# Moving borders between six mixers: an earlier first rounding of the second mixture call, a one-hot add at the end of the expert-choice mixer, and a new spread of jobs in a quaternion attention loop

## The reference

```python
x = x + 0.5 * _L0_ffn_ref(_layernorm(x), ...)    # top-2 of 7 experts, and a shared one
x = x + _L0_attn_ref(_layernorm(x), ...)         # 16 heads, 64 landmarks, 6 steps of an iterative inverse
x = x + 0.5 * _L0_ffn_ref(_layernorm(x), ...)
x = x + 0.5 * _L1_ffn_ref(_layernorm(x), ...)    # 16 experts choose their tokens, after 6 Sinkhorn steps
x = x + _L1_attn_ref(_layernorm(x), ...)         # quaternion projections, softmax attention
x = x + 0.5 * _L1_ffn_ref(_layernorm(x), ...)
```

```python
out = out.at[jnp.arange(b)[:, None, None], idx].add(gates[..., None] * expert_out)
```

## Time and profile before

| | us |
|---|---|
| median of 3 runs (lowest, highest) | 2918.04 (2917.66, 2918.88) |
| the profiled execution | 2915.34 |
| its span in the trace | 2913.6 |
| PE, DVE, ACT, POOL busy | 2781.3, 1843.2, 1635.9, 543.7 |

### The profile page before, as it was taken

How to read it: one execution, slowest core, us unless ns; L and a number is a source line. 1 busy time by engine, 2 the same in 40 slices (tenths; PEclk the granted TensorE clock), 3 DMA queues, 4 the chain that set the end, 5 groups by cost and what they waited for, 6 DMA issues and landing times.

```text
span 2913.6 us, 55420 instructions
## 1 busy us (share of the span) xinstructions
PE 2781.3 (95%) x22813; PEld 2168.1 (74%) x22813; DVE 1843.2 (63%) x3741; ACT 1635.9 (56%) x2473; POOL 543.7 (19%) x478
## 2 busy tenths in 40 slices
PE   9999999997999999999999978998999999998998
PEld 7889999996767778889999956995333434333998
DVE  7775555548887687755545477785635463436776
ACT  4534555543443355344545434775798878892776
POOL 0002224121000000022232254553000000001343
PEclk9999999998999999999999989999999999998999
DMA  4213333232000022233333354774442252513675
GB/s 157 71 66 124 83 87 98 70 86 73 2 2 24 3 69 80 66 113 92 85 84 87 79 155 128 206 201 104 98 131 54 71 112 64 124 38 119 190 205 139
DMA packets 237853, 279.72 MB, mean 96 GB/s; under 512 B 23811, under 2 KB 219040, under 8 KB 237600
## 3 DMA queue, kind: packets, MB, share of 16 engines
q1 hardware_dynamic: 205296, 228.75, 26.8%
q0 software_dynamic: 30720, 45.85, 8.1%
q10 hardware_dynamic: 1584, 1.57, 0.2%
HBM read 204.58 MB, written 72.88 MB: 95 GB/s over the span
## 4 chain that ended last, share of the span: by engine, by line
PE 74%; DVE 15%; ACT 5%; issue 4%; DMA 2%; POOL 1%; DVEq 0%; POOLq 0%; ACTq 0%
PE PS L162 17%; PE PS L163 16%; PE PS L164 16%; PE PS L2960 13%; PE PS L1043 6%; PE PS L170 2%; DVE SM L194 1%; ACT FW L556 1%; ACT Z L600 1%; DVE SM L1418 1%; PE PS L502 1%; DVE PROD L628 1%; DVE FW L640 1%; PE PS L3053 1%; PE PS L178 1%
## 5 line engine op out<-in xcount | busy, mean ns | idle before, releaser
L3110 ACT ACTIVATE P<-PS 128x1024 f32<-128x1024 f32 x512 | 484.9, 1046 | 94.8 <-PE PS L2960 93.1
L162 PE MATMUL PS<-FH,FW 128*128 128x366 f32 (+1 forms) x1408 | 506.5, 360 | 5.6 <-ACT SIL L542 4.3
L163 PE MATMUL PS<-FH,FW 128*128 128x366 f32 (+1 forms) x1408 | 497.5, 353 | 0.0
L164 PE MATMUL PS<-FH,FW 128*128 128x366 f32 (+1 forms) x1408 | 495.3, 352 | 0.0
L550 ACT ACTIVATE FHH<-PROD 128x366 fp32r<-128x366 f32 (+1 forms) x352 | 194.4, 552 | 424.1 <-DVE PROD L628 423.8
L162 PE MATMUL PS<-FW,FHH 128*122 128x256 f32 (+1 forms) x1184 | 337.8, 285 | 1.5 <-DVE FHH L635 1.5
L163 PE MATMUL PS<-FW,FHH 128*122 128x256 f32 (+1 forms) x1184 | 333.9, 282 | 0.0
L164 PE MATMUL PS<-FW,FHH 128*122 128x256 f32 (+1 forms) x1184 | 332.8, 281 | 0.0
L628 DVE TENSOR_TENSOR PROD<-SIL,PS 128x366 f32<-128x366 f32 (+1 forms) x352 | 206.9, 588 | 165.6 <-PE PS L164 155.8
L635 DVE TENSOR_TENSOR FHH<-PROD,FHH 128x366 fp32r<-128x366 f32 (+1 forms) x352 | 208.9, 594 | 147.4 <-ACT FHH L550 147.2
L162 PEld LDWEIGHTS PS<-FH,FW 128*128 128x128 f32 x1408 | 264.7, 188 | 30.5 <-ACT SIL L542 8.1
(11 more groups left out here) (468 smaller groups left out, 5562.4 us busy)
## 6 DMA issues: line engine op xcount, KB each, us to landing
WS<-L_ffn_w_dram SPq DMA_DIRECT2D x256, 256.0 KB, 3.7
WST<-L_ffn_W_dram SPq DMA_DIRECT2D x168, 256.0 KB, 3.4
S<-parts_scratch SPq DMA_DIRECT2D x60, 384.0 KB, 8.1
parts_scratch<-PT SPq DMA_DIRECT2D x28, 512.0 KB, 4.5
WST<-L_ffn_W1s_dram SPq DMA_DIRECT2D x40, 256.0 KB, 2.8
WST<-L_ffn_W3s_dram SPq DMA_DIRECT2D x40, 256.0 KB, 3.4
WST<-L_ffn_W2s_dram SPq DMA_DIRECT2D x40, 256.0 KB, 4.0
xa_scratch<-X SPq DMA_DIRECT2D x17, 512.0 KB, 5.1
```

The costliest lines, as they stand in the source:

```text
L162: e.matmul(o, lh, rh, start=start, stop=False, skip_group_check=True)
L163: e.matmul(o, ll, rh, start=False, stop=False, skip_group_check=True)
L164: return e.matmul(o, lh, rl, start=False, stop=stop, skip_group_check=True)
L3110: e.activation(self.PR[K % 3][:, 2 * jj:2 * jj + 2, :].rearrange("p a b -> p (a b)"), c.pair(2 * ((2 * K + jj) % 3)), ACT.Exp, scale=0.25) ...
```

## The change

**Opening.** X's first row group and the first weight piece are issued first, row groups 0, 2, 3 and 4 to 7 all on SP; g, b and the router's weights `WRF` move to ACT's queue. The 13 products of ones, 8 before the transposes and 5 behind, become 11 and 2.

**Second Ffn0 call.** `FW` gets a fixed place at the top of memory (the halves swap roles: `fw(q)` is half (q+1)%2), so it doesn't lie under tiles that Attn0 still uses; Attn0's `WP` moves. Seven pieces, no longer two, run ahead in Attn0's tail: loads and half of the statistics, the other half, root's first step, its other steps, the norm of rows 0 to 3, of rows 4 to 7, and the first weight rounding `wt 0` (between the last two and the last `le` items). The 2 products of ones before the second call's transposes go. `Z` and `FW` wait for batch 3's last use of what lay there (`rows_free`). g and b are not loaded a second time.

```diff
@@ Ffn0.order
-        self.ahead = [[("ld", n, 0), ("ld", n, 1), ("stats", n, 0, 4)], [("stats", n, 4, 8)]]
-        seq = [("consts", n), *self.ahead[0], *self.ahead[1], ("root", n, 0, 8)]
-        seq += [("norm", n, i, i + 4) for i in (0, 4)] + [("wt", n, 0), ("fill", n, 8 if self.first else 2)]
-        seq += [("tp", n, h, c) for h in range(2) for c in range(2)] + [("fill", n, 5 if self.first else 3), ("lg", n, 0)]
+        self.ahead = [[("ld", n, 0), ("ld", n, 1), ("stats", n, 0, 4)], [("stats", n, 4, 8)], [("root", n, 0, 8, 0)],
+                      [("root", n, 0, 8, 1)], [("norm", n, 0, 4)], [("norm", n, 4, 8)], [("wt", n, 0)]]
+        seq = [("consts", n)] + [it for piece in self.ahead for it in piece]
+        seq += [("fill", n, 11)] * self.first
+        seq += [("tp", n, h, c) for h in range(2) for c in range(2)] + [("fill", n, 2 if self.first else 3), ("lg", n, 0)]
@@ Attn0.__init__
-        self.rooms = ("lc", call, 3, 0, 0), ("le", call, 3, 3)
+        self.rooms = (("ib", call, 2, 0, 4), ("nd", call, 3, 1), ("ld", call, 2, 0, 0), ("iw", call, 3, 1), ("ld", call, 2, 1, 1),
+                      ("le", call, 2, 2), ("le", call, 3, 3))
+        c.rows_free = last(*values, *[("qk", call, 3, *x) for x in ALL4])
@@ macaron_kernel
-        parts.append((opens, begin[:5]))
+        parts.append((opens, begin[:3]))
-                own[:1] = [(ph, head[:3]), (opens, begin[5:]), (ph, head[3:])]
+                own[:1] = [(ph, head[:2]), (opens, begin[3:5]), (ph, head[2:3]), (opens, begin[5:]), (ph, head[3:])]
```

```diff
+            if not self.final and k == 59:
+                seq.append(("oh", n))
+            if not self.final and k == 61:
+                seq.append(("xget", n, 0))
...
-        return seq + [("end", n) if self.final else ("xget", n, 0)]
+        return seq + ([("end", n)] if self.final else [("hot", n, y) for y in range(4)])
@@ pe
+        elif k == "hot":
+            w.wait_ge(*p.at("oh", ("oh", n)))
+            w.wait_ge(*p.at("yev", ("ye", n, 15), 1))
+            for t in range(2):
+                o_ = 128 * (2 * it[2] + t)
+                ins = e.matmul(self.pb(it)[:, 256 * t:256 * t + 256], self.OH[0:64, o_:o_ + 128], self.YE[1][0:64, 0, :],
+                               start=True, stop=True, skip_group_check=True)
@@ dve
+        elif k == "hot":
+            w.wait_ge(*p.at("xl4" if y >= 2 else "xl0", ("xget", n, 0)))
+            w.wait_ge(*p.at("hp", it))
+            e.tensor_tensor(rows, rows, self.pb(it).rearrange("p (i d) -> p i d", i=2), ALU.add).then_inc(*p.one("hv"))
@@ sp, xget
-            w.wait_ge(*p.at(f"sc{b // 2}", ("sc", n, 15)))
+            w.wait_ge(*p.at(f"sc{b // 2}", ("sc", n, 15 if b else 14)))
```

```diff
@@ prep
+        to_rows, to_second, each_turned, each_query = {1: (8, 1, (2, 2, 2, 2), 2), 2: (4, 2, (1, 1, 1, 1), 1),
+                                                          3: (5, 1, (2, 1, 1, 1), 1)}[b]
-        q.add(5, ("zz", n, b, 0))
-        q.add(1, ("zz", n, b, 1), ("xb", n, b))
+        q.add(to_rows, ("zz", n, b, 0))
+        q.add(to_second, ("zz", n, b, 1), ("xb", n, b))
@@ sink_stats
-            q.add(1, *[("stats", self.call, b, b, i + x) for x in range(2)])
+            q.add(5 if b == 1 and not i else 1, *[("stats", self.call, b, b, i + x) for x in range(2)])
```

More of the change, by code:

```diff
@@ L198, in stats, with root @@
         ins.then_inc(*p.one("dv"))
-    def root(self, e, w, gs, done, by=1.0, more=EPS):
+    def root(self, e, w, gs, done, by=1.0, more=EPS, steps=(0, 1, 2)):
         p = self.p
@@ L205, in root @@
         w.wait_ge(*p.mine())
-        e.tensor_scalar(s1, self.MV[:, gs, 1], by, more, ALU.mult, ALU.add).then_inc(*p.one("dv"))
-        w.wait_ge(*p.mine())
-        e.tensor_scalar(s2, s1.bitcast(U32), -0.5, 1597463007.0, ALU.mult, ALU.add).then_inc(*p.one("dv"))
-        w.wait_ge(*p.mine())
-        e.tensor_copy(o.bitcast(U32), s2).then_inc(*p.one("dv"))
-        w.wait_ge(*p.mine())
-        for n in range(3):
+        if 0 in steps:
+            e.tensor_scalar(s1, self.MV[:, gs, 1], by, more, ALU.mult, ALU.add).then_inc(*p.one("dv"))
+            w.wait_ge(*p.mine())
+            e.tensor_scalar(s2, s1.bitcast(U32), -0.5, 1597463007.0, ALU.mult, ALU.add).then_inc(*p.one("dv"))
+            w.wait_ge(*p.mine())
+            e.tensor_copy(o.bitcast(U32), s2).then_inc(*p.one("dv"))
+            w.wait_ge(*p.mine())
+        for n in steps:
             e.scalar_tensor_tensor(s3, o, -0.5, o, ALU.mult, ALU.mult).then_inc(*p.one("dv"))
@@ L398, in order @@
                 if j == 2 and ui == last:
-                    seq += [("xget", n, q) for q in (7, *range(7))]
+                    seq += [("xget", n, q) for q in ((0, 1, 7, *range(2, 7)) if self.first else (7, *range(7)))]
                 if e_ is not None and j == 1 and e_ + 2 < E0:
@@ L550, in act @@
             e.activation(self.FHH[:, s % 2, 0, hs], self.PROD[:, h, 0:NH], ACT.Copy).then_inc(*p.one("hi"))
+        elif k == "consts":
+            if self.first:
+                for x, name in enumerate(("g", "b")):
+                    e.dma_start(c.GB[:, x, :], c.A[f"L0_ffn_ln_{name}"].rearrange("(c p) -> p c", p=128),
+                                allow_slow_non_contiguous=True).then_inc(*p.dma("gb"))
+                self.router_weights(e, w, it)
         elif k == "wt":
@@ L555, in act @@
                 w.wait_ge(*p.at("dn", ("down", n, 2 * q - 3)))
-            e.activation(self.FW[:, q % 2, 0, :], self.WST[:, q % 2, :], ACT.Copy).then_inc(*p.one("wh"))
+            elif self.rows_free:
+                w.wait_ge(*p.at(*self.rows_free))
+            e.activation(self.fw(q)[:, 0, :], self.WST[:, q % 2, :], ACT.Copy).then_inc(*p.one("wh"))
         elif k in ("tp", "xt"):
@@ L648, in dve @@
         elif k == "root":
-            c.root(e, w, slice(*it[2:]), "dv", 1.0 + EPS, EPS * EPS)
+            steps = ((0,), (1, 2))[it[4]] if len(it) > 4 else (0, 1, 2)
+            c.root(e, w, slice(*it[2:4]), "dv", 1.0 + EPS, EPS * EPS, steps)
         elif k == "norm":
             w.wait_ge(*p.mine())
+            if it[2] < 8 and self.rows_free:
+                w.wait_ge(*p.at(*self.rows_free))
             for i in range(it[2], it[3]):
@@ L2056, in __init__ @@
         if not final:
-            c.xsrc = {i: ("xl4" if 4 <= i < 8 else f"xl{i // 8}", ("xget", call, i // 8)) for i in range(NT)}
+            c.xsrc = {i: (f"xl{i // 8}", ("xget", call, i // 8)) for i in range(8, NT)}
             c.scattered = [(f"sc{bb}", ("sc", call, 15)) for bb in range(2)]
@@ L2407, in pool @@
                     w.wait_ge(*p.at(f"sc{bb}", ("sc", n, e_ - 1)))
+                if e_ == 15 and bb == 0 and not self.final:
+                    for name in ("xl0", "xl4"):
+                        w.wait_ge(*p.at(name, ("xget", n, 0)))
                 e.indirect_dma_start(
@@ L2745, in start @@
         rest.add(1, ("vv", n, 0, 2))
-        rest.add(1, ("sta", n, 0, 0, 1), ("sta", n, 0, 1, 1), ("put", n, 0), ("stk", n, 1))
+        rest.add(1, ("sta", n, 0, 0, 1))
+        rest.add(1, ("sta", n, 0, 1, 1), ("put", n, 0), ("stk", n, 1))
         rest.add(1, ("vv", n, 0, 3), ("xb", n, 0))
@@ L2808, in sink_jobs @@
             if self.on_pe(it):
-                q.add(1, *job)
+                q.add(2 if b == 0 and it == ("zg", n, 0, 0, 0) else 1, *job)
                 job = []
@@ L3397, in sp @@
         c, p = self.c, self.c.p
-        if it[0] == "xload" and it[1] not in (1, 2, 3):
+        if it[0] == "xload" and it[1] != 1:
             self.xload(e, it[1])
```

67 lines of the change are left out of this document (44 added, 23 removed), and 2 rows, old and new, of the table COUNTS.

## The result

| | before | after |
|---|---|---|
| median of 4 runs (lowest, highest), us | 2917.85 (2916.54, 2918.88) | 2885.19 (2883.06, 2888.61) |
| the profiled execution (span) | 2915.34 (2913.6) | 2888.61 (2886.9) |
| ratio, 95% interval | | 0.9896 (0.9884, 0.9907) |

Faster by 1.04%, 32.7 us in the medians and 26.7 in the traces. The forecast was 2898, a gain of 19.7, with a range that ended at 2890. The direction was right, and the size too small. Of the four runs of the kernel after, the profiled one is the slowest and has the lowest mean granted clock (0.986; the others have 0.988, 0.990 and 0.988), which goes with the smaller gain in the traces.

The account below looks back on a forecast made before the run. TensorE, busy 95% of the span, was taken as the bound; opening 3.3, border 5.1, mixer's end 4.2 and loop 7.1 sum to 19.7 us, so 2918.0 becomes 2898, range 2890 to 2909.

Parts of the forecast that it names:

- Opening: Start of the kernel: with ones moved ahead of the transposes, first product at about 18.7, a gain of 3.3 us.
- the loop's term: Quaternion loop: PE's waits at job turns and half clock go, net 7.1 us, bounds -2 and 9.
- The rival that the clock stays low: Both first-mixture borders: transposes and following passes stay at half clock, 4.4 us back, 2903 us; chance 0.11.
- Border: Start of the second first-mixture call: first product 5.8 us earlier, tail cost 0.65, net gain 5.1 us.
- Mixer's end: Expert-choice mixer's end: load no longer waits for scatter 15, one-hot products instead; statistics 4.3 earlier, net 4.2 us.
- Gone should be: Loop: waits for transposed halves 4.0, L170 1.3, `S` 1.3 and half clock 1.5 vanish, 8.1 us.
- charge of 1.0: Loop: cost for new small waits, with batch 2's root and norms pressed together in turns 73 to 76.
- 1.5 behind turn 144: Loop: the half-clock stretch from 2390 to 2392 after the stop at turn 144 goes, worth 1.5 us.
- No wait of over 0.5 us on L3255: Sign of being right, in the loop: PE never waits over 0.5 us for the copy of a transposed half.
- all terms near their best: Whole kernel: lower end of the forecast's range, 2890 us.
- The slower rival: Loop: batch 1's stack comes late and stops turn 64, time 2925 us or more; chance 0.03.
- The loop gives nothing: Loop: its waits are replaced by others of the same size, time 2905 us; chance 0.15.

Follow-up runs that it names:

- `top_no_swap`: Kernel before with only FW's place moved to the top of memory, halves not swapped; first-mixture calls of 654.62 and 651.50 us.
- second pair: Kernels before and after, both unchanged, run again on one chip; medians 2916.84 and 2887.18 us, ratios 0.9998 and 0.9901.
- `ctl_before`: Kernel before, unchanged, run again for a second trace; median 2916.84 us, ratio 0.9998 to the kernel before.
- `gate_stats_old`: Changed kernel with batch 1's gate statistics starting after one turn, not five; turns 128 to 192 take 157.8 us.
- `no_loop`: Changed kernel with all of the loop's schedule as before; ratio 0.9930 to the kernel before.
- `loop_only`: Kernel before with the whole new loop schedule alone; ratio 0.9958 to the kernel before.

## Why the prediction was too small

Two steps of the sum failed: the loop's term was too small (7.1; it was 10.8 and 12.6), and the move of `FW` had no term at all (the first-mixture calls gained 2.8). The other three terms held.

*Opening: right.* 3.5 against 3.3, first product at 18.47 against 18.7, transposes 1.91 at full clock against 2.2. The rival that the clock stays low is out: the first product stands between 17.97 and 18.62 in all nine traces with 11 ones ahead. Against an execution of the kernel before whose clock does not fall the gain is near 2.2.

*Border: right, a little small.* 5.88 between the last output product and the first real one, a gain of 6.3 against 5.8, and the tail pays 0.8 against 0.65. The transposes took 1.97 against 2.2 and nothing was late next.

*Mixer's end: right.* 4.2 against 4.2 in the way to turn 0, statistics 0.8 us behind the last product of the one-hot.

*FW's place: put at nothing.* I took the buffer's move as a precondition for the pieces ahead, and by "time is to be had only where PE stands still, where it does ones or work at half clock" I shut out that PE's own products could take another time. Each call gained 1.4, 2.8 in all, of which `top_no_swap` shows 1.2 to 2.1 to be the place.

*Loop: the mechanism right, the sum wrong in three places.* "Gone should be" 8.1 less a charge of 1.0. In the first pair of traces 10.8 went: 7.4 of idle time, 1.5 by one stretch at 0.50 less (two before, one after), and 1.9 of other busy time. In the second pair 12.6 went: 7.7, 3.1 by two such stretches, and 1.9. First, the charge of 1.0 for batch 2's new order had the wrong sign: at equal clock it gained 1.4. Second, the waits that I counted were not all that went: with batch 3's gate statistics in the old place the stretch costs 5.0 (`ctl_before`) to 5.8 (`gate_stats_old`) at full clock, where I had counted 1.7 and 1.3. Two small waits on the copies of an output (OC, 0.8) and on later halves came with them, and the other busy time. Third, I counted half clock once, 1.5 behind turn 144. It is there in four of the six traces with the old loop and in none of the ten with the new one. But each of the six has one or two more in turns 0 to 64, to which I gave nothing; the kernel before has one from 2038 us on in the very trace that I read (0.53 from 2038 to 2040).

*The signs named ahead.* Full clock in the transposes, statistics within 0.6 us of the last addition (0.1), full clock behind turn 144 and no wait at turn 64 are all there. "No wait of over 0.5 us on L3255" is not: the 1.9 ahead of `zt` is one. The first product of the second call stands at 1035.61, and the sign asked for 1041.9 - 3.3 + 0.65 = 1039.3. 1.5 of the difference is the first call, which had no term, and 1.4 the Nystrom stage, which moves by more than that between executions.

*The range.* It ended at 2890, "all terms near their best". The best bounds named, 4.0, 6.5, 4.8 and 9, add up to 24.3 us and give 2893.7, so even they don't reach the 2885.2 that was measured. The 1.9 us for moving the first weight piece follows from no row, and a turn of two exponentials is 1.82 and not 1.86 by the earlier trace rows; neither changes the forecast.

*What remains.* Terms shown: 3.5 + 5.5 + 4.2 + 2.8 + 10.8 = 26.8 us. With the loop of the second pair, 12.6, it is 28.6. The ratios say 30.3 (27.1 to 33.8) and 28.9 (24.2 to 33.6) us, the medians 32.7 and 30.9. So 26.8 lies just below the first interval and inside the second, and 28.6 inside both. The kernel after meets less half clock over all: in the second pair of timings its mean granted clock is 0.9872 (four runs) against 0.9846 (17 runs). How much of that is in stages that the change doesn't touch would need many traces of both.

The slower rival had no part: nothing waits at turn 64, and `stk 4` is not on any list. "The loop gives nothing" is refuted by `no_loop` and `loop_only`.
